# Layer 0's first four groups gathered during the node stage, a gather ring of eight, logit products in two halves

## The chip, the cores and the metric

The kernel runs on one core of one Trainium2 chip. The metric is the device time of one execution in microseconds; the time of a kernel is the median of several executions.

## The reference

Two graph layers over 12500 nodes (128 features, fp32) and 200000 edges that are sorted by destination:

```
xl, xr = x @ W_l, x @ W_r                       # by node; heads: 4 x 32
e      = sum_c leaky_relu(xl[src] + xr[dst]) * att
p      = exp(e - max over dst)                  # with a self loop for each node
out    = segment_sum(p / denom * xl[src], dst) + bias + x
x1     = layernorm(x + layernorm(out) * gamma + beta)
neigh  = segment_sum(x1[src] + edge_attr, dst)  # layer 1
out    = layernorm(x1 + leaky(( 2*x1 + neigh) @ W1 + b1) @ W2 + b2)
```

## The kernel before, in words

**Node stage.** 100 blocks of 128 nodes are handled in 50 pairs. SyncE loads x, TensorE turns it (`across`) and multiplies it with `w_lr` (`product`), ScalarE copies out, VectorE makes the self logits, SyncE stores `xl_table` (xl and four linear numbers for each node, DW = 132 wide) and `xr_table`. GpSimd prepares constants and then adds four numbers to `e_self` for each pair (`add_linear`).

**Sweep of layer 0.** The edges lie in 196 groups of 1024 (8 tiles of 128; the last group has 3 tiles), 1563 tiles in all. For each tile GpSimd issues one indirect DMA that gathers 128 rows of `xl_table` into `rows[s]`, a ring of U = 4 groups; it waits for the group's source numbers (`src_in0`) and for the slot (`rows_free0`, which VectorE gives in `weigh`). For each group TensorE turns the gathered rows (`sources`), adds the target rows by a one-hot product (`targets`, L804), multiplies with the attention vectors (`attend`, L830), and sums the weighted rows of the group before (`sum_up`, L846), which needs VectorE's one-hot (`edge_one_hot`, L1247). VectorE does the running maxima (`maxima`, `across`, `shift`) and the weighting (`weigh`, L1214). In every fourth group a window of 256 nodes is merged and written to `x1_table` (`merge_*`). Each engine has its own program, written out for four groups in a hardware loop (`sweep`), and the engines meet in semaphores alone. The order of TensorE in one step is: `sources(g+1)`, the turns of the maxima, `targets(g+1)`, `sum_up(g-1)`, `attend(g+1)`.

**Layer 1.** The same walk over 196 groups, with gathers of `x1_table` (L1588), behind a barrier of all engines.

Of the kernel before, what the change touches and what calls it, by code (L numbers as in the profile page):

```python
# [50 lines left out]
AHEAD = 3  # L51
# [39 lines left out]
def sweep(eng, groups, step, ends=None, layer=0, back=1):  # L91

    def part(tag, j, first, steps, lo, n):
        regs = []
        if ends is not None:
            regs = [eng.alloc_register(f"ends{layer}_{tag}_{k}") for k in range(2 * n)]
            eng.load(regs, ends[0:1, bass.ds(2 * first if j is None else j * (2 * U), 2 * n)])
        for c in steps:  # L100
            step(Group(j, c), lambda g: (regs[2 * (g.c - lo)], regs[2 * (g.c - lo) + 1]))

    part("head", None, 0, range(back), 0, max(2, back))
    with eng.Fori(0, groups // U - 1) as j:
        part("body", j, 0, range(back, U + back), 0, U + max(2, back))
    base = groups - U
    part("tail", None, base, range(base + back, groups + back), base, U)
# [67 lines left out]
def build(nc, a, out, edges, groups, blocks):  # L175
    nodes, real = blocks * P, REAL
    pairs = blocks // 2
    assert groups % U == 0 and groups > U and pairs % UP == 0 and pairs > UP
# [10 lines left out]
    with ctx:  # L189
# [48 lines left out]
        src_idx = [sb(f"src_idx{s}", [P, T], I32) for s in range(U)]  # L238
# [42 lines left out]
        near_row = pT2[:, T * NA:T * NA + P]  # L281
# [36 lines left out]

        row_slots = slots(rows[0]) + slots(rows[1]) + slots(rows[2]) + slots(rows[3])
# [22 lines left out]
        with nc.Block() as block:  # L342
            @block.sync
            def _(sp):
                for t, n in ((w_lr[:, 0:D], "W_l"), (w_lr[:, DW:DW + D], "W_r")):
                    sp.dma_start(t, a[n]).then_inc(S("products_in"), 16)

                def load(q):
                    if q.at_least(2 * R):
                        sp.wait_ge(S("x_taken"), q.times(1, 1 - 2 * R))  # L350
                    s = q.c % (2 * R)
                    sp.dma_start(ring_x[s], x_pair[q.times(1)]).then_inc(S(f"x_in{s}"), 16)

                def store(q):
                    s = q.c % R
                    if q.j is None and q.c < AHEAD:
                        sp.dma_start(src_idx[q.c][:, :], bass.AP(a["src"].tensor, q.c * G, [[T, P], [1, T]]))\
                          .then_inc(S(f"src_in0{q.c}"), 16)
# [10 lines left out]
            def _(pool):  # L369
# [29 lines left out]
                def add_linear(q):  # L399
                    pool.wait_ge(S("self_summed"), q.times(1, 1))  # L400
                    e_of = e_self_pair[:, q.times(1)]
                    pool.tensor_tensor(e_of, e_of, ring_w[q.c % R][:, :, D:DW], ALU.add).then_inc(S("e_made"), 1)

                node_loop(pool, pairs, [(add_linear, 0)])
# [33 lines left out]
            def _(act):  # L438
# [22 lines left out]
                def copy_out(q):  # L461
                    s = q.c % R
                    act.wait_ge(S("lr_ready"), q.times(1, 1))
                    if q.at_least(R):
                        act.wait_ge(S(f"xl_out{s}"), q.use(16, 0, R))
                        act.wait_ge(S("e_made"), q.times(1, 1 - R))
# [9 lines left out]
            def _(v):  # L476
# [51 lines left out]
                v.wait_ge(S("e_made"), pairs)  # L528
# [46 lines left out]
        def merge_of(g):  # L575

            return Group(g.j, (g.c - 1) // U, 1)
# [46 lines left out]
        def weights_in(v, k0, k1, link):  # L624
# [4 lines left out]
            tmp, own, self_ = msets[:, k0:k1, at_tmp:at_tmp + 2 * H], pair[:, :, 0, :], pair[:, :, 1, :]  # L629
            link(v.tensor_scalar(by_node(tmp), den, 0.0, -BIG, ALU.is_le, ALU.mult))  # L630
            link(v.tensor_tensor(by_node(own), su[:, :, :, H * HC:WC], by_node(tmp), ALU.add))
# [60 lines left out]
        def load_sources(sp, g):  # L692

            s, n = g.c % U, tiles(g)
            sp.wait_ge(S("src_taken0"), g.times(1, 2))
# [3 lines left out]
        with nc.Block() as block:  # L699
            @block.sync  # L700
            def _(sp):
                base, n, n_more, home = (sp.alloc_register(r) for r in ("sp_base", "sp_n", "sp_n_more", "sp_home"))
                sp.reg_mov(n_more, 0)

# [4 lines left out]
                def step(g, near):  # L709
# [34 lines left out]
                    if g.at_least(1) and not (g.j is None and g.c + AHEAD - 1 >= groups):  # L744
                        load_sources(sp, g + (AHEAD - 1))

# [5 lines left out]
                for s in range(BACK):  # L752
                    sp.wait_ge(S(f"rows_free0{s}"), groups // U + 1)
                    sp.dma_start(src_idx[s][:, :], bass.AP(a["src"].tensor, s * G, [[T, P], [1, T]]))\
# [3 lines left out]
            def _(pool):  # L758
                tables_stored(pool, ("xl",))
                def gather(s, n):  # L760
                    for t in range(n):
                        pool.indirect_dma_start(rows[s][:, t, 0:DW], None, xl_table[:, :],  # L762
                                                bass.IndirectOffsetOnAxis(ap=src_idx[s][:, t:t + 1], axis=0))\
# [7 lines left out]
                for s in range(U):  # L771
                    wait_alone(pool, pool_waits, S(f"src_in0{s}"), 16 * (groups // U))
                    wait_alone(pool, pool_waits, S(f"rows_free0{s}"), groups // U)
                    gather(s, tiles(Group(None, groups - U + s)))

            @block.tensor
            def _(pe):
# [10 lines left out]
                def sources(g):  # L788

                    s, h = g.c % U, ph[0]  # L790
                    wait_alone(pe, pe_waits, S(f"gathered0{s}"), g.use(16 * T, 16 * tiles(g)))
                    if g.at_least(1):
                        pe.wait_ge(S("relu_ready"), g.times(2, 0))
                    for t in range(tiles(g)):
                        pe.matmul(h[:, t, :], rows[s][:, t, 0:D], ident[:, :], start=(t % 4 == 0), stop=False,  # L795
# [26 lines left out]
                def attend(g):  # L822

                    if g.at_least(1):
# [1118 lines left out]
```

## Time and profile before

| | |
|---|---|
| median of 3 runs | 4075.12 us (4073.79 to 4075.89) |
| profiled execution: time | 4078.24 us |
| profiled execution: span of the trace | 4076.4 us |
| node stage | until 77 us |
| gathers of layer 0 | 77.5 to 2044 us |
| gathers of layer 1 | 2098 to 4062 us |
| busy share PE / DVE / ACT / GpSimd | 75% / 52% / 39% / 73% |
| granted TensorE clock, mean | 0.892 |

The shares are averages over three stages with different limits, so they don't say what bounds any of them. What counts is the spacing of GpSimd's gathers, and who waits for whom in each stage.

### The profile page before, as it was taken

What the parts mean: (1) busy time and instruction counts of PE and PEld (TensorE: products, weight loads), DVE (VectorE), ACT (ScalarE), POOL (GpSimd) and SP (SyncE); (2) the same over time, 40 slices, a digit from 0 to 9 for tenths busy, and PEclk for the clock granted to TensorE, in tenths of its full rate; (3) what the DMA queues carried; (4) which work ended last, traced back from release to release, by engine and by line L of the source; (5) the groups of instructions that cost most, each with busy time, mean ns of one, the idle gap of its engine ahead of it and who ended that gap; (6) DMA issues with size and microseconds to landing.
All of it is one profiled execution on the core that took longest, in us unless ns stands there. A gap on an engine that the chain in (4) does not pass through costs nothing. (4 is left out here: it accounts for less than half of the span.)

```text
span 4076.4 us, 80602 instructions
## 1 busy us (share of the span) xinstructions
PE 3042.1 (75%) x19237; PEld 2546.8 (62%) x19238; DVE 2101.4 (52%) x8183; ACT 1598.5 (39%) x3438; POOL 2993.8 (73%) x3200
## 2 busy tenths in 40 slices
PE   7888888888888888888846666666666666666666
PEld 6666666666666666666636666565666665666665
DVE  6777777777777777777743222222222222322222
ACT  5555555555565655555612212112121212121111
POOL 3777777777777777777737777777777777777776
PEclk9999999999999999999978888888888888888888
DMA  7545455554555454545444444444444444444443
GB/s 232 141 130 137 133 136 133 135 133 133 135 134 137 132 135 130 135 130 136 131 89 124 117 118 117 117 117 122 118 117 117 117 118 119 121 117 118 117 117 92
DMA packets 446506, 518.24 MB, mean 127 GB/s; under 512 B 198373, under 2 KB 346536, under 8 KB 446472
## 3 DMA queue, kind: packets, MB, share of 16 engines
q1 hardware_dynamic: 266390, 268.21, 21.7%
q0 software_dynamic: 100032, 208.27, 21.5%
q10 hardware_dynamic: 80050, 41.37, 3.6%
q8 instruction: 14, 0.23, 0.0%
q14 instruction: 20, 0.16, 0.0%
HBM read 470.23 MB, written 47.29 MB: 127 GB/s over the span
## 5 line engine op out<-in xcount | busy, mean ns | idle before, releaser
L1588 POOL DMA_INDIRECT rows<-x_table,src_idx x1563 | 1487.3, 952 | 530.0 <-issue 530.0
L762 POOL DMA_INDIRECT rows<-xl_table,src_idx x1563 | 1489.6, 953 | 479.0 <-issue 456.7
L846 PE MATMUL pA<-wmsg,edge_of 128*128 128x136 f32 x3126 | 405.6, 283 | 123.7 <-DVE edge_of L1247 123.1
L989 ACT ACTIVATE relu_h<-ph 128x512 f32<-128x512 f32 x391 | 231.3, 597 | 616.0 <-PE ph L804 616.0
L1611 PE MATMUL pA<-edge_of,dst_row 128*128 128x128 f32 x1568 | 304.0, 373 | 226.1 <-DMA rows<-x_table,src_idx 215.9
L846 PEld LDWEIGHTS pA<-wmsg,edge_of 128*128 128x128 f32 x3126 | 379.1, 190 | 134.5 <-issue 131.6
L1718 ACT ACTIVATE relu_h<-ph,b 128x128 f32<-128x128 f32 x196 | 72.0, 367 | 976.3 <-PE ph L1668 864.0
L1611 PEld LDWEIGHTS pA<-edge_of,dst_row 128*128 128x128 f32 x1568 | 283.4, 279 | 241.6 <-issue 240.9
L1611 PE MATMUL pT<-node_of,dst_row 128*128 128x128 f32 x1558 | 294.4, 367 | 181.2 <-DMA rows<-x_table,src_idx 172.1
L804 PE MATMUL ph<-node_of,xr_win 128*128 128x512 f32 (+1 forms) x782 | 411.8, 652 | 7.0 <-issue 6.6
L1044 ACT ACTIVATE node_of<-dst_row,first_node 128x1024 f32<-128x1024 int32 x196 | 405.5, 2069 | 2.4 <-DVE first_node L1158 2.4
L1611 PEld LDWEIGHTS pT<-node_of,dst_row 128*128 128x128 f32 x1558 | 274.1, 273 | 196.1 <-issue 195.2
L830 PE MATMUL pT<-att_heads,relu_h 128*128 128x48 f32 x3126 | 368.2, 271 | 0.0
L830 PEld LDWEIGHTS pT<-att_heads,relu_h 128*128 128x128 f32 x3126 | 364.6, 192 | 5.4 <-ACT relu_h L989 0.6
L795 PE MATMUL ph<-ident,rows 128*128 128x128 f32 x1563 | 225.6, 291 | 132.2 <-DMA rows<-xl_table,src_idx 131.5
L1663 PE MATMUL ph<-ident,relu_h 128*128 128x128 f32 x196 | 66.0, 337 | 326.5 <-DVE relu_h L1833 274.9
L1828 DVE TENSOR_TENSOR xr<-xr,pA 128x128 f32 x98 | 28.3, 288 | 540.2 <-PE pA L1611 537.3
L795 PEld LDWEIGHTS ph<-ident,rows 128*128 128x128 f32 x1563 | 180.7, 148 | 182.9 <-issue 181.1
L1247 DVE TENSOR_TENSOR edge_of<-dst_rel,pT 128x1024 f32<-128x1024 f32 x196 | 238.7, 1218 | 96.6 <-DVE dst_rel L1244 85.3
L1798 DVE TENSOR_TENSOR node_of<-sums,ph 128x1024 f32<-128x1024 f32 x98 | 119.0, 1214 | 274.8 <-issue 205.8
L1663 PEld LDWEIGHTS ph<-ident,relu_h 128*128 128x128 f32 x196 | 27.7, 141 | 363.6 <-DVE relu_h L1833 303.9
L1051 ACT ACTIVATE node_of<-node_of,one 128x1024 f32<-128x1024 f32 x196 | 224.5, 1145 | 61.5 <-issue 61.4
(207 smaller groups left out, 5454.4 us busy)
## 6 DMA issues: line engine op xcount, KB each, us to landing
dst_row<-in_dst SPq DMA_DIRECT2D x195, 513.0 KB
dst_row<-in_edge_attr SPq DMA_DIRECT2D x195, 512.0 KB
rows<-xl_table,src_idx POOLq DMA_INDIRECT x1563
rows<-x_table,src_idx POOLq DMA_INDIRECT x1563
sums_table<-win ACTq DMA_DIRECT2D x196, 68.0 KB
xr_win<-xr_table SPq DMA_DIRECT2D x196, 64.0 KB
relu_h<-x_table SPq DMA_DIRECT2D x196, 64.0 KB
out_x<-relu_h ACTq DMA_DIRECT2D x193, 64.0 KB
```

The lines of the kernel that those rows point to most:

```text
L762: pool.indirect_dma_start(rows[s][:, t, 0:DW], None, xl_table[:, :], bass.IndirectOffsetOnAxis(ap=src_idx[s][:, t:t + 1], axis=0))\
L795: pe.matmul(h[:, t, :], rows[s][:, t, 0:D], ident[:, :], start=(t % 4 == 0), stop=False, is_transpose=True)
L804: return [pe.matmul(h[:, k:min(k + 4, tiles(g)), :], xr_of[:, :], by_tile[:, k:min(k + 4, tiles(g)), :], start=False, stop=stop) for k in ...
L830: ins = pe.matmul(out_t[:, t, :], relu_h[0][:, t, :], att_heads[:, :], start=(t == 0), stop=(t == tiles(g) - 1))
L846: ins = pe.matmul(pA[k][:, 0:WC], edge_of[k][:, t, :], w[:, t, :], start=(t == 0), stop=(t == tiles(g) - 1))
L989: act.activation(relu_h[0][:, k:to, :], ph[0][:, k:to, :], ACT.Relu, scale=1.0 - GAT_SLOPE)\
L1044: act.activation(in_tiles(node_of[g.c % 2], tiles(g)), ids, ACT.Abs, scale=-1.0, bias=first_node[:, s:s + 1])\
L1051: act.activation(of, of, ACT.Relu, scale=-1.0, bias=one[:, :]).then_inc(S("node_of_made"), 1)
L1247: one_hot = lambda k: v.tensor_tensor(edge_of[k][:, 0:n_of, :], dst_rel[:, 0:n_of].unsqueeze(2).to_broadcast([P, n_of, P]), near_row.unsqu ...
L1588: pool.indirect_dma_start(rows[s][:, t, 0:D], None, x1_table[:, :], bass.IndirectOffsetOnAxis(ap=src_idx[s][:, t:t + 1], axis=0))\
L1611: ins = pe.matmul(bank, m[:, t, :], one_hot[:, t, :], start=(k == 0 and t == 0), stop=(k == 1 and t == n - 1))
L1798: return v.tensor_tensor(of[:, 0:n, :], rel[:, 0:n].unsqueeze(2).to_broadcast([P, n, P]), row_bank.unsqueeze(1).to_broadcast([P, n, P]), A ...
```

## The change

The source numbers of groups 0 to 3 are loaded at the very start. In the node stage GpSimd no longer runs `add_linear`; behind its constants it gathers the rows of **x** (not of `xl_table`) for groups 0 to 3, 32 indirect DMAs into `pre_rows`, a part of the tile `sums`. At the head of layer 0, TensorE and VectorE turn these rows and multiply them with `w_lr[:, 0:132]` in 16 pairs of tiles, and VectorE writes the products back over the rows. GpSimd's gathers from `xl_table` begin with group 4. `pre_rows` then serves as four more slots: the ring is eight deep (RING = 8), and so is the ring of source numbers. The loops of the sweep are written out for eight groups, not four. `attend` is split: the first four tiles' products are issued ahead of `sum_up`, the last four behind it. The linear part of the self logit is added by VectorE in the merge (one instruction more in `weights_in`). `near_row` moves from PSUM tile `pT2` to `ph[1]`, with two waits of VectorE on the merge.

```diff
-                def add_linear(q):
-                    pool.wait_ge(S("self_summed"), q.times(1, 1))
-                    ...
+                for k in range(U):
+                    pool.wait_ge(S(f"src_in0{k}"), 16)
+                    for t in range(T):
+                        pool.indirect_dma_start(pre_rows[:, k, t, 0:D], None, a["x"][:, :],
+                                                bass.IndirectOffsetOnAxis(ap=src_idx[k][:, t:t + 1], axis=0))\
+                            .then_inc(S(f"gathered0{U + k}"), 16)
```

```diff
+                for k in range(U):
+                    load_numbers(k)
...
-                with pool.Fori(0, groups // U - 1) as j:
-                    for s in range(U):
-                        wait_alone(pool, pool_waits, S(f"src_in0{s}"), j * 16 + 16)
-                        wait_alone(pool, pool_waits, S(f"rows_free0{s}"), j + 1)
-                        gather(s, T)
+                with pool.Fori(0, (groups - U) // RING - 1) as j:
+                    for c in range(U, U + RING):
+                        gather(Group(j, c, RING))
```

```diff
-                for _ in range(24):
-                    pe.matmul(pA[0][:, 0:P], ident[:, :], ident[:, :], start=True, stop=True)
+                def turn_pre(k):
+                    ...
+                    for b in range(2):
+                        ins = pe.transpose((pT1, pT2)[k % 2][:, b * P:(b + 1) * P], pre_rows[:, g, t + b, 0:D], ident[:, :])
+                def multiply_pre(k):
+                    ...
+                    for b in range(2):
+                        ins = pe.matmul(lr_bank[k % 2][:, b, 0:DW], pre_x[k % len(pre_x)][:, b, :], w_lr[:, 0:DW],
+                                        start=True, stop=True)
+                for k in range(len(pre_pairs) + 1):
+                    if k < len(pre_pairs):
+                        turn_pre(k)
+                    if k >= 1:
+                        multiply_pre(k - 1)
...
+                    if beyond:
+                        attend(g + 1, 0)
                     if g.at_least(1):
                         sum_up(g + -1, near(g + -1))
                     if beyond:
-                        attend(g + 1)
+                        attend(g + 1, 1)
```

```diff
+                def convert(first, last):
+                    for k in range(first, last):
+                        if k < len(pre_pairs):
+                            v.wait_ge(S("x_taken"), pairs + k + 1)
+                            v.tensor_copy(pre_x[k % len(pre_x)], (pT1, pT2)[k % 2][:, 0:2 * P]...)
+                        if k >= 1:
+                            v.wait_ge(S("lr_ready"), pairs + k)
+                            v.tensor_copy(pre_rows[:, g, t:t + 2, 0:DW], lr_bank[(k - 1) % 2][:, :, 0:DW])
...
                     if not g.at_least(1):
+                        half = len(pre_pairs) // 2
+                        convert(0, half + 1)
                         prepare(g)
                         first_of(g)
+                        convert(half + 1, half + 5)
                         homes_of_merges()
                         first_of(g + 1)
+                        convert(half + 5, 2 * half + 1)
                         starts_of_steps()
...
+                    if merge_phase(g) == 1:
+                        v.wait_ge(S("m_b_normed"), merge_of(g).times(1, 1))
```

## Rows read from the trace of the kernel before

**Rows 1.** The page: costliest groups; busy, mean ns | idle before, releaser.

```profile
L762 POOL DMA_INDIRECT rows<-xl_table,src_idx x1563 | 1489.6, 953 | 479.0 <-issue 456.7
```

**Rows 2.** Instructions of L762, with first and last start, and what ended its idle time.

```profile
L762 POOL DMA_INDIRECT rows<-xl_table,src_idx x1563: 947/952/1257, 77.5 to 2043.2; - x196
...
  DVE wmsg L1214: 9.8, 32
```

**Rows 3.** Instructions on the tile rows: ns min/median/max, first and last start.

```profile
L795 PE MATMUL ph<-ident,rows x1563: 272/273/472, 92.0 to 2053.3; 128*128 128x128 f32 x196
...
L1588 POOL DMA_INDIRECT rows<-x_table,src_idx x1563: 947/952/1628, 2098.2 to 4060.6; - x196
```

**Rows 4.** Waits from 140 to 2040 us: who for whom, total us, times, longest.

```profile
PE pA L846 <- DVE edge_of L1247: 121.8, 123, 1.1
PE ph L795 <- DMA rows<-xl_table,src_idx: 117.5, 103, 1.9
```

**Rows 5.** Windows: length, busy PE PEld DVE ACT POOL, clock, DMA share, GB/s.

```profile
40.00:60.00 20.00, 18.80 (x94) 14.55 (x93) 17.59 (x47) 14.29 (x46) 3.00 (x15) 1.00 0.81 250
...
80.00:100.00 20.00, 12.44 (x68) 10.18 (x66) 5.11 (x29) 8.21 (x9) 15.16 (x16) 0.76 1.03 301
...
500.00:1000.00 500.00, 434.39 (x2751) 329.56 (x2751) 371.69 (x1558) 293.37 (x607) 378.71 (x399) 0.97 0.51 134
```

**Rows 6.** Timeline of GpSimd, node stage and start of layer 0: start, us.

```profile
13.65 0.90 POOL L396 COPY att_heads<-att_col 32x1 f32<-32x1 f32 x4
...
77.49 1.21 POOL L762 DMA_INDIRECT rows<-xl_table,src_idx  x1 [1.93 <-issue]
...
109.21 0.95 POOL L762 DMA_INDIRECT rows<-xl_table,src_idx  x1 [1.32 <-DMA src_idx<-in_src]
```

**Rows 7.** Timeline, first microseconds of the kernel.

```profile
1.64 3.75 SPq L352 DMA_DIRECT2D rows<-in_x  x8
...
5.43 0.44 SPq L357 DMA_DIRECT2D src_idx<-in_src  x1
...
5.54 1.10 PE L415 MATMUL pT<-ident,rows 128*128 128x128 f32 x4 [5.54 <-DMA rows<-in_x]
```

**Rows 8.** The page's DMA queues: packets, MB, share of 16 engines.

```profile
q0 software_dynamic: 100032, 208.27, 21.5%
...
q8 instruction: 14, 0.23, 0.0%
q14 instruction: 20, 0.16, 0.0%
```

**Rows 9.** Node stage, 0 to 78 us: a wait, and a store's time to landing.

```profile
ACT edge_of L467 <- DMA xl_table<-edge_of: 1.8, 3, 1.2
...
xl_table<-edge_of SPq DMA_DIRECT2D x50, 132.0 KB, 2.6
```

**Rows 10.** Timeline, end of the node stage and head of layer 0.

```profile
63.78 0.41 DVE L513 TENSOR_TENSOR dst_row<-edge_of,ph 128x256 f32<-128x256 f32 x1
...
64.18 0.38 PE L415 MATMUL pT<-ident,rows 128*128 128x128 f32 x2
...
64.39 1.06 PE L428 MATMUL ph<-w_lr,rows 128*128 128x260 f32 x4
...
76.95 8.25 PE L882 MATMUL pA<-ident 128*128 128x128 f32 x48 [4.03 <-PEq L342]
...
92.04 1.94 PE L795 MATMUL ph<-ident,rows 128*128 128x128 f32 x8 [6.19 <-DMA rows<-xl_table,src_idx]
...
108.16 0.16 DVE L1158 TENSOR_TENSOR first_node<-node_id,firsts 128x1 f32<-128x1 f32 x1 [2.43 <-DMA dst_row<-in_dst]
...
110.74 1.22 DVE L1214 TENSOR_TENSOR wmsg<-rows,pT 128x1024 f32<-128x1024 f32 x1 [0.89 <-ACT r_exp L1028]
```

**Rows 11.** Timeline, a merge's instruction and a slot's sources in mid sweep.

```profile
1042.61 0.17 DVE L631 TENSOR_TENSOR sums<-sums 128x8 f32<-128x8 f32 x1
...
1046.20 1.07 PE L795 MATMUL ph<-ident,rows 128*128 128x128 f32 x8 [1.17 <-DMA rows<-xl_table,src_idx]
```

More of the change, by code:

```diff
@@ L50 @@
 TAIL = 3
-AHEAD = 3
+RING = 2 * U
 class Group:
@@ L91, in sweep, with part @@
 def sweep(eng, groups, step, ends=None, layer=0, back=1):
-    def part(tag, j, first, steps, lo, n):
+    pool = []
+    def part(j, first, steps, lo, n):
         regs = []
         if ends is not None:
-            regs = [eng.alloc_register(f"ends{layer}_{tag}_{k}") for k in range(2 * n)]
-            eng.load(regs, ends[0:1, bass.ds(2 * first if j is None else j * (2 * U), 2 * n)])
+            while len(pool) < 2 * n:
+                pool.append(eng.alloc_register(f"ends{layer}_{len(pool)}"))
+            regs = pool[0:2 * n]
+            eng.load(regs, ends[0:1, bass.ds(2 * first if j is None else j * (2 * RING), 2 * n)])
         for c in steps:
[L101 to L107, printed above, removed]
+            step(Group(j, c, RING), lambda g: (regs[2 * (g.c - lo)], regs[2 * (g.c - lo) + 1]))
+    loops = (groups - back - (RING - 1)) // RING
+    done = RING * loops
+    part(None, 0, range(back), 0, max(2, back))
+    with eng.Fori(0, loops) as j:
+        part(j, 0, range(back, RING + back), 0, RING + max(2, back))
+    part(None, done, range(done + back, groups + back), done, groups - done)
 def walk(eng, tag, groups, step, back, extra=0, wants=(), unrolled=0):
@@ L177, in build @@
     pairs = blocks // 2
-    assert groups % U == 0 and groups > U and pairs % UP == 0 and pairs > UP
+    assert groups % U == 0 and groups > 2 * RING and (groups - U) % RING == 0 and pairs % UP == 0 and pairs > UP
     assert nodes - 2 * UP * P <= real <= nodes - SPAN
@@ L317, in slots, with row_slot @@
                     for k in range(0, G - 2 * width + 1, 2 * width)]
+        assert U * PITCH <= 3 * groups
+        pre_rows = sums[:, :, :].rearrange("p b k -> p (b k)")[:, 0:U * T * PITCH].rearrange("p (s t k) -> p s t k", s=U, t=T)
+        rows_of_slot = [t[:, :, :] for t in rows] + [pre_rows[:, s] for s in range(U)]
+        pre_pairs = [(g, t) for g in range(U) for t in range(0, T, 2)]
+        pre_x = [relu_h[1][:, t:t + 2, :] for t in range(0, T, 2)]
+        def row_slot(g):
+            return (g.c + U) % RING
         row_slots = slots(rows[0]) + slots(rows[1]) + slots(rows[2]) + slots(rows[3])
@@ L703, in _ @@
                 sp.reg_mov(n_more, 0)
+                for k in range(U):
+                    sp.wait_ge(S(f"gathered0{U + k}"), 16 * T)
                 def window(first):
@@ L794, in sources @@
                     for t in range(tiles(g)):
-                        pe.matmul(h[:, t, :], rows[s][:, t, 0:D], ident[:, :], start=(t % 4 == 0), stop=False,
+                        pe.matmul(h[:, t, :], rows_of_slot[s][:, t, 0:D], ident[:, :], start=(t % 4 == 0), stop=False,
                                   is_transpose=True)
```

116 lines of the change are left out of this document (68 added, 48 removed).

## Prediction

> **What bounds the kernel now.** I read the page's costliest groups first, then the two gather lines by themselves, then the waits of the layer 0 stretch, and last the timelines where the stages meet. The costliest line of layer 0 is GpSimd's gather [rows 1]: its 1563 instructions keep the engine busy for 953 ns each, and nearly all of the idle time between them is "issue", which means that GpSimd waited for nobody. The source view says the same with a first and a last start [rows 2]: 1562 steps in 2043.2 - 77.5 = 1965.7 us, or 1.258 us a tile and 10.07 us a group of eight. Only 32 of them followed a wait for VectorE's `weigh`, 0.3 us each, no longer than the usual pause. So from 77.5 us on the sweep is as long as GpSimd's list of gathers. Layer 1 has the same list once more [rows 3] and isn't touched.
>
> The other engines have a little room. From 140 to 2040 us, some 189 groups, TensorE waited 117.5 us for gathered rows, 0.62 us a group, and 121.8 us (0.64 us a group) for the one-hot ahead of `sum_up` [rows 4]. Without the first wait a group would take them about 9.45 us. TensorE is busy 434 of 500 us there and VectorE 372 [rows 5], so the room isn't large.
>
> **The change part by part.**
>
> *32 gathers leave the list.* Groups 0 to 3 are 32 tiles, 32 x 1.258 = 40.3 us. If the first `xl_table` gather still starts at 77.5 us and GpSimd never waits, the last one starts 40.3 us earlier. What follows the last gather (layer 1's first gather starts 55 us behind it [rows 2, 3]) hangs on the last groups and merges, and moves along if the other engines have caught up by then. They have: at 9.45 us a group, 196 groups from about 105 us end near 1960 us, ahead of GpSimd's new end near 2005 (2043.2 less this term, and the others below). Term: -40.3.
>
> *The numbers of group 4.* GpSimd waited 1.32 us for them once [rows 6], against the usual 0.3. With eight slots they are loaded long before. Term: -1.0.
>
> *Source numbers at the start.* Four loads now stand in SyncE's queue ahead of the first load of x. One takes 0.44 us to issue [rows 7], so the first x starts 1.76 us later, and TensorE's first turn waited for exactly that load until 5.54 us [rows 7]. Nothing hides it; the node stage then runs at VectorE's pace and doesn't make it good. Term: +1.7 (0 if the ramp absorbs it, 2.0 at most). Four more loads stand ahead of the first stores; the stores' ring of five pairs covers them.
>
> *32 gathers in the node stage.* GpSimd is through its constants at 14.5 us [rows 6] and then has nothing but `add_linear`, 3.0 of 20 us [rows 5], which goes. 32 x 1.258 = 40.3 us, so it is done near 55 us, 22 us ahead of need. The cost is DMA traffic. The gathers' queue took 21.5% of 16 engines' span for 3126 gathers [rows 8], or 0.28 us of all engines for each. Spread at 1.258 us that adds 0.22 to a share of 0.81 [rows 5], which makes 1.03. The head of layer 0 shows just that share, at 301 GB/s against 250 here [rows 5], so it can be carried, but landings get longer. A store lands after 2.6 us, the ring gives it five pairs (about 6 us), and so far ScalarE waited 1.8 us in all for one [rows 9]. Bounds: 0, and 32 x 0.28 = 9.0 us if the engines were full and every gather pushed the stage back. I take +1.5, near the lower end, since the observed wait is small.
>
> *The product at layer 0's head.* A pair of tiles takes TensorE two turns (0.38 us) and two products of 132 columns, half of the 260-column pair's 1.06 us [rows 10], so 0.9 us; at the low clock of this stretch (mean 0.76 [rows 5]) up to twice that: the turns of eight tiles at 92 us took 1.94 us, in mid sweep 1.07 [rows 10, 11]. VectorE has two copies of about 0.42 us each (as L513 for 256 columns [rows 10]). With hand-overs I take 1.1 us a pair, 1.4 over the first four, and 3 us for VectorE's own head work in between: 77 + 16 x 1.2 + 3 = 99 us. TensorE's cover goes: the 24 warming products (8.25 us [rows 10]) and the wait for the first gather until 92.0 us were idle time that this fills. From there `sources(0)`, `targets(0)`, `attend(0)`, the maxima and `shift` take about 13 us, so `weigh(0)` ends near 112 us. The step before also ended there for another reason: VectorE waited for `dst_row` until 108.16 us and `weigh(0)` ran from 110.74 to 111.96 [rows 10]; that load stands behind the stores of `xr_table` in SyncE's program, as it will after the change. GpSimd needs slot 4 free only for its 33rd gather, at 77.5 + 40.3 = 117.8 us. So 6 us are spare. Term: 0, with bounds 0 and +8 (at 2 us a pair `weigh(0)` ends at 125 us).
>
> *Half the products ahead of `sum_up`.* Four tiles' products now run in the 0.64 us a group in which TensorE waits for the one-hot [rows 4]. That shortens TensorE's step by up to as much, but GpSimd sets the pace. Term: 0 in the sweep.
>
> *One more instruction in the merge* (0.17 us and its wait [rows 11], about 0.2) lies in one step of four, within the room; once it is behind the last group: +0.2. VectorE's new wait for `m_b_normed` is for work that ScalarE does at the end of its step before, and VectorE gets to the place only behind TensorE's turns of the next step: 0; what is queued behind it is the one-hot, for which TensorE's `sum_up` waits. If room were gone, 49 x 0.2 = 10 us would be the bound.
>
> *Loops of eight groups.* The profile counts 1558 VectorE instructions in 500 us [rows 5], 31 a group; a pass of eight has 250, and semaphore, register and branch instructions on top. The code that a loop needs is fetched once today: 34 packets of instructions in the whole span [rows 8], against 48 passes of each loop. What a jump costs when code isn't there is bounded by TensorE's 4.03 us at the entry into layer 0 [rows 10]. In 23 passes, one of 80.5 us each, a stall of 4.03 us meets room of 8 x 0.62 = 5.0 us. Term: 0.
> The Trainium skill (Runtime: NRT & Kernel Launch, section Instruction fetch mechanics) says that an engine other than TensorE holds 512 instructions, and that a taken branch out of that window stalls for a fetch. By it VectorE's pass of eight, if it holds over 512, would stall at each back edge where the pass of four shows no fetch; the trace of before has no loop that long and can't decide it. The sum would be the same as long as the room covers the stall.
>
> **Sum.** -40.3 - 1.0 + 1.7 + 1.5 + 0.2 = -37.9 us. The profiled execution took 4078.2 us (span 4076.4 and 1.8 around it), which gives 4040.3. The median of the runs shown is 3.1 us below that execution, so I forecast 4075.1 - 37.9 = 4037.2, say 4037 us.
>
> **Rivals.**
> - *Late handover.* VectorE and TensorE need 1.7 to 2.2 us a pair, `weigh(0)` ends after 118 us and GpSimd waits up to 8 us at its 33rd gather: 4038 to 4045. For it: the low clock at the head, and a chain of four hand-overs a pair. Against: 6 us of spare time.
> - *The node stage is pushed back* by the added traffic, 3 to 9 us in place of 1.5: 4039 to 4045. For it: share 0.81 before. Against: 1.03 was carried elsewhere.
> - *The list of gathers isn't what matters*: the other engines can't go faster than 10.07 us a group, and the head start is lost, since their last step comes when it came. 4075, no change. The 117.5 us of TensorE's waits for gathers speak against it.
> - *A stall in each pass of the longer loops* (slower). VectorE or TensorE fetches code at each back edge. It costs nothing up to 5 us a pass, and 23 us for each further microsecond; 37.9 / 23 = 1.65, so from 6.7 us a pass on the kernel is slower than before. At 8 us, two stalls as at the entry: 4037 + 69 = 4106. Against it: one such stall is 4 us, and the halved products leave TensorE another 0.6 us a group.
>
> **How the numbers follow.** Forecast as summed (4030 to 4043): 0.61. Late handover 0.13. Node stage pushed back 0.13. A stall that eats part of the gain (4045 to 4067) 0.04. No change 0.04, slower by the stall 0.05. What a measurement of this kernel can tell from no change is about 0.2%, 8 us. Faster takes the first three and most of the fourth, 0.90; within 0.2% 0.05; slower 0.05. The first rivals together reach 4053; below 4030 nothing in the sum leads (no start-up loss and no traffic cost give 4034). Range 4030 to 4054.
>
> **What the profile will show.** 1531 gathers from `xl_table`, first near 79 to 81 us (the node stage is 1.7 + 1.5 us longer), 1.258 us apart, last start near 2005 us. Layer 1's first gather 55 us behind it. 32 gathers of x between 15 and 56 us. TensorE's waits for gathered rows in the sweep no smaller than before, and its wait for the one-hot nearly gone. GpSimd waits for `weigh` at most once. Wrong if: GpSimd shows waits for `weigh` in each pass; a gap in VectorE's or TensorE's list every 80 us with instruction packets beside it; or the first `xl_table` gather starts past 85 us.

## The result, and the profile after

The changed kernel takes 4108.87 us (median; 4108.34 to 4116.3), the kernel before took 4074.45 us beside it: ratio 1.0088, 95% interval 1.0071 to 1.0106. It is 34 us slower. 4037 had been forecast, so 72 us are to be explained. The profiled execution is the slowest of the four (4116.3 us, span 4114.7), 7 us above the median, so differences of spans and starts between the two profiles come out some us larger than the 34.

First GpSimd's gathers, with first and last start, and what ended GpSimd's idle time (the name is that of the tile that holds the slot):

```profile
L789 POOL DMA_INDIRECT rows<-xl_table,src_idx x768: 947/952/1121, 81.5 to 2008.2; - x192
L789 POOL DMA_INDIRECT sums<-xl_table,src_idx x763: 946/952/1206, 121.9 to 2042.2; - x191
...
  issue: 484.9, 1445
  DVE wmsg L1274: 39.7, 86
```

There are 1531 gathers from `xl_table` in place of 1563, and the first starts at 81.5 us, near the 81 forecast. But the last starts at 2042.2 us, where it was before [rows 2], not near 2005. The list is 32 gathers shorter and as long in time. GpSimd now waits for VectorE's `weigh` 86 times. The logits, and layer 1's first gather (2098.2 us before [rows 3]), show that the layer as a whole ends later still:

```profile
L1262 DVE TENSOR_TENSOR logits<-pT,sums x100: 164/202/205, 105.0 to 2099.6; 128x32 f32<-128x32 f32 x99, 128x12 f32<-128x12 f32 x1
```

```profile
L1658 POOL DMA_INDIRECT rows<-x_table,src_idx x1563: 947/952/2234, 2137.4 to 4100.8; - x196
```

195 steps in 1994.6 us are 10.23 us a group. Before, the same line ran from 98.7 to 2062.3 us, 10.07 a group. Layer 1 is 39 us later at its start and 1 us longer in itself. So nearly all of the loss in these two profiles lies in layer 0's sweep (31 us) and ahead of it (6 us).

Who waits for whom there, 140 to 2040 us (total us, times, longest), against [rows 4]:

```profile
PEld pT L951 <- DVE run L1266: 130.6, 82, 4.1
DVE logits L1262 <- issue: 126.3, 23, 5.8
PE pT L951 <- DVE run L1266: 107.3, 78, 3.9
```

TensorE's waits for gathered rows and for the one-hot have gone from the head of the list. In their place it waits for `run`, the softmax scan of VectorE, and VectorE stands 23 times, 5.5 us each, ahead of the logits with nothing in the profile that it waits for. There are 23 passes of the longer loop. In the kernel before this row read 63.0 us in 47 times, 1.3 us each (reading a pass's registers and branching). The timelines of VectorE, ScalarE and TensorE around one of the 23:

```profile
1020.82 0.17 DVE L702 SCALAR_TENSOR_TENSOR sums<-sums 128x2 f32<-128x2 f32 x1
1026.59 0.20 DVE L1262 TENSOR_TENSOR logits<-pT,sums 128x32 f32<-128x32 f32 x1 [5.60 <-issue]
```

```profile
1022.71 0.34 ACTq L1017 DMA_DIRECT2D x_table<-sums  x1
1028.14 0.37 ACTq L629 DMA_DIRECT2D sums<-sums_table  x1
```

```profile
1022.47 1.97 PE L818 MATMUL ph<-ident,sums 128*128 128x128 f32 x8 [1.96 <-issue]
1027.36 0.37 PE L951 MATMUL pT<-ident,run 128*4 128x128 f32 x1 [2.93 <-DVE run L1266]
...
1028.01 3.78 PE L827 MATMUL ph<-node_of,xr_win 128*128 128x512 f32 x4
...
1038.65 1.55 PE L827 MATMUL ph<-node_of,xr_win 128*128 128x512 f32 x3 [0.19 <-issue]
```

VectorE's last instruction of the pass starts at 1020.82 us and the first of the next at 1026.59. The views leave out branches and register loads, but the trace has their records: VectorE's branch back ends at 1021.35 us, its next record of any kind starts at 1024.97, and the load of the pass's registers takes another 1.35 us. This gap behind the branch, 3.6 us in the median of 23 passes (2.7 us on ScalarE, 0.1 on TensorE), is what "gap" means below; before the change it is 0.3 us on VectorE and 0.2 on ScalarE. ScalarE issues nothing between 1023.1 and 1028.1 us. TensorE runs out of work and waits for `run`; after that the four matmuls of `targets` take 3.78 us; three of them take 1.55 us at the full clock (last line), so four need about 2. Windows around this stall (length, busy PE, granted clock, DMA share, GB/s) show why: in the second the clock is at the lower of its two levels (1.2 GHz in place of 2.4), behind TensorE's two waits, and in the third at the upper one again.

```profile
1012.00:1020.00 8.00, 7.53 (x52) 1.00 0.52 152
1025.00:1032.00 7.00, 4.58 (x8) 0.50 0.44 110
1036.00:1044.00 8.00, 7.44 (x43) 1.00 0.46 123
```

What came in the meantime is in the DMA queues, packets and MB, of the whole page and of the window 300 to 1000 us:

```profile
q14 instruction: 296, 2.42, 0.2%
q8 instruction: 23, 0.38, 0.0%
```

```profile
q14 instruction: 99, 0.81, 0.4%
```

99 packets of instructions in mid sweep, 8.2 KB each, about 12 for each pass of 82 us. Before, the same window had none, and the whole span 34 [rows 8]. This is the rival "A stall in each pass of the longer loops", and two of the prediction's three signs of being wrong are there: waits for `weigh` in each of five passes looked at, and VectorE's gap every 80 us with instruction packets beside it. The third isn't, since the first gather starts before 85 us.

What a pass pays shows in the steps from the start of one group's logits to the next, by their place in the pass (means of 21 passes). Before, the step that holds VectorE's branch took 11.8 us. Now it takes 15.8, 4 us more, and the step in the middle of the pass, which no longer has a branch and a load of registers, takes 10.1, 1.6 us less. So the stall arrives in full, and the longer loop gives back a good third of it.

### The profile page after: what moved, and what is told of

It reads as the page before. It is cut to its first block and busy times, and to the rows that moved or that the text cites. A ratio compares the mean times of both kernels' runs of the same rounds, so it can differ in the third digit from the quotient of the medians.

```text
span 4114.7 us, 79626 instructions
## 1 busy us (share of the span) xinstructions
PE 3116.4 (76%) x19285; PEld 2585.2 (63%) x19286; DVE 2115.6 (51%) x8265; ACT 1601.8 (39%) x3438; POOL 2990.2 (73%) x3150
## 5 line engine op out<-in xcount | busy, mean ns | idle before, releaser
L789 POOL DMA_INDIRECT sums<-xl_table,src_idx x763 | 732.1, 960 | 263.6 <-issue 234.6
L789 POOL DMA_INDIRECT rows<-xl_table,src_idx x768 | 732.2, 953 | 261.0 <-issue 250.3
L827 PE MATMUL ph<-node_of,xr_win 128*128 128x512 f32 (+1 forms) x782 | 429.2, 676 | 17.0 <-issue 11.0
L870 PE MATMUL pA<-wmsg,edge_of 128*128 128x136 f32 x3126 | 419.7, 289 | 6.6 <-DVE edge_of L1307 5.6
L853 PE MATMUL pT<-att_heads,relu_h 128*128 128x48 f32 x3126 | 411.5, 276 | 12.9 <-ACT relu_h L1041 12.9
L853 PEld LDWEIGHTS pT<-att_heads,relu_h 128*128 128x128 f32 x3126 | 392.9, 196 | 25.3 <-ACT relu_h L1041 13.8
L870 PEld LDWEIGHTS pA<-wmsg,edge_of 128*128 128x128 f32 x3126 | 387.5, 195 | 13.8 <-issue 8.3
L1307 DVE TENSOR_TENSOR edge_of<-dst_rel,ph 128x1024 f32<-128x1024 f32 x196 | 238.7, 1218 | 104.6 <-DVE dst_rel L1304 104.6
L827 PEld LDWEIGHTS ph<-node_of,xr_win 128*128 128x128 f32 x782 | 146.1, 208 | 165.6 <-issue 149.8
```

The lines of the kernel that those rows point to most:

```text
L789: pool.indirect_dma_start(rows_of_slot[s][:, t, 0:DW], None, xl_table[:, :], bass.IndirectOffsetOnAxis(ap=src_idx[k][:, t:t + 1], axis=0))\
L827: return [pe.matmul(h[:, k:min(k + 4, tiles(g)), :], xr_of[:, :], by_tile[:, k:min(k + 4, tiles(g)), :], start=False, stop=stop) for k in ...
L853: ins = pe.matmul(out_t[:, t, :], relu_h[0][:, t, :], att_heads[:, :], start=(t == 0), stop=(t == tiles(g) - 1))
L870: ins = pe.matmul(pA[k][:, 0:WC], edge_of[k][:, t, :], w[:, t, :], start=(t == 0), stop=(t == tiles(g) - 1))
L1307: one_hot = lambda k: v.tensor_tensor(edge_of[k][:, 0:n_of, :], dst_rel[:, 0:n_of].unsqueeze(2).to_broadcast([P, n_of, P]), near_row.unsqu ...
```

## The experiments

The instructions of a pass, counted in the programs: VectorE 314 before and 619 after, ScalarE 158 and 310, TensorE 327 and 644 (752 and 1494 with a matmul in fp32 counted as several). A pass holds more than it executes: `further_windows` is a loop for groups that span several windows, and its body, never entered with these inputs, stands in the code as often as the group does.

**Shorter loops, one engine and then all.** Edit: the `further_windows` loops of layer 0 are left out, so that groups that span several windows would not be computed; in the first run VectorE's two alone, in the second also ScalarE's, TensorE's and SyncE's.

```diff
                     wait_alone(v, v_waits, S("first_made"), g.times(1, 1))
-                    further_windows(v, n, span, further)
...
-                    further_windows(v, n, span, further)
                     one_hot(0).then_inc(S("edge_of_made"), 1)
```

> The changed kernel with the never-entered inner loops for groups wider than 128 nodes taken out of VectorE's layer 0 program alone (leaves out the handling of such groups; these inputs have none). VectorE's pass of eight groups shrinks from 619 to 386 instructions in the program; what it executes is nearly the same. Theory A (the pass of eight is too long for what VectorE holds, so it fetches code and stalls at each back edge, about 5 to 6 us in every 82 us pass): VectorE's gap at the back edge goes, GpSimd sets the pace again, 4030 to 4050 us. Theory B (other engines' step got longer through the split products, the moved near_row and the merge's extra instruction): 4100 to 4110, as the changed kernel. Theory C (it is ScalarE's or TensorE's longer pass that stalls): 4090 to 4110.

> The same inner loops taken out of all engines' layer 0 programs (VectorE 386, TensorE 965 in place of 1494, ScalarE 210 in place of 310, SyncE 88 in place of 176 instructions a pass; leaves out the handling of groups wider than 128 nodes, of which these inputs have none). Theory A: the same as with VectorE's alone, 4030 to 4050 us, unless 386 instructions still don't fit for VectorE. Theory C: this one is fast, 4030 to 4050, and the one with VectorE's alone is not. Theory B: 4095 to 4110.

Measured: VectorE alone (386 instructions a pass) 4090.4 us, ratio 1.0036 (1.0022 to 1.005); all engines (VectorE 386, ScalarE 210, TensorE 965, again with matmuls counted as several) 4056.43 us, 0.9939 (0.9918 to 0.996). In 300 to 1000 us the packets fall from 99 to 83 and 44:

```profile
q14 instruction: 83, 0.68, 0.3%
```

```profile
q14 instruction: 44, 0.36, 0.2%
```

Leaving these loops out of all engines moves the time by 52 us, and the second kernel is faster than the one before. Not all of it is shorter code. The register and branch instructions around the loops go too: their busy time falls from 1.12 to 0.39 us a group on TensorE and from 1.04 to 0.59 on VectorE. And 386 instructions aren't short enough for VectorE: behind its branch back there is still a gap of 2.95 us (3.6 in the changed kernel), and yet this kernel is as fast as the one below in which no engine stalls. How the 52 us divide between stall and register work isn't shown by these two runs. ScalarE's gap of 2.8 us is there with 310 instructions and gone with 210. The Trainium skill (Runtime: NRT & Kernel Launch, section Instruction fetch mechanics) gives these engines 512 instructions, refilled in blocks of 256, and a stall for a taken branch out of that window. The stall is as the page has it. As a limit on the length of a loop the 512 don't hold here, since loops of 386 and 310 are stalled; the packets are of 8.2 KB, half of the page's 16 KiB blocks. Where in a block each loop begins was neither recorded nor varied, so what the limit depends on isn't shown.

**The long loop without the change.** Edit: the kernel before, with 38 (then 16) memsets in each of VectorE's eight never entered bodies. No instruction more is executed.

```diff
                         v.reg_add(n_hide, n_hide, 1)
+                        for _ in range(38):
+                            v.memset(warm[:, :], 0.0)
...
                         v.reg_add(n_sum, n_sum, 1)
+                        for _ in range(38):
+                            v.memset(warm[:, :], 0.0)
```

> The kernel before, with 38 memsets put into each of VectorE's eight never-entered inner loops of layer 0: nothing more is executed, only the code of a pass of four groups grows from 314 to 622 instructions. Theory A: instruction packets appear in every pass of 40 us, VectorE stalls 5 to 6 us at each back edge, room is 2.5 us, so a pass becomes 43 to 44 us and the kernel takes 4074 + 48 x 3 to 4, 4200 to 4270 us. Theory B: 4074, no change.

> The same with 16 memsets in each: 446 instructions a pass. Theory A with a limit of 512 instructions: no instruction packets in the loop and 4074 us, no change; if the code is held in blocks and the pass now touches one block too many, as slow as the longer one (4200 to 4270). Theory B: 4074.

Measured: 622 instructions a pass, 4231.39 us, 1.0379 (1.0362 to 1.0397); 446 a pass, 4201.78 us, 1.0309 (1.0292 to 1.0326). Their loops have 48 passes, so the price is (4231.4 - 4076.5) / 48 = 3.2 us and 2.6 us a pass. In 300 to 1000 us there are 113 and 82 instruction packets where the kernel before has none, and the gap behind VectorE's branch is 2.9 and 3.0 us in place of 0.3. The wait of the long one, and its gathers:

```profile
DVE logits L1204 <- issue: 177.0, 44, 4.4
```

```profile
L762 POOL DMA_INDIRECT rows<-xl_table,src_idx x1563: 946/952/1214, 77.4 to 2194.1; - x196
```

4.0 us each in place of 1.3, so the stall itself is 2.7 us, and all or nearly all of it arrives in the time of both (the step with the branch takes 14.7 and 14.5 us in place of 11.8). That the two prices differ by 0.6 us at the same gap isn't explained. The kernel before had no room for a stall either. The gathers that were to set the pace were themselves held back, from 2043 to 2194 us.

**A hint for the branch.** Edit: in the changed kernel the branches back of VectorE's and ScalarE's loops of eight groups are announced by a prefetch hint. In the trace it is the first instruction of each pass, so it stands some 80 us ahead of the branch that it announces.

```diff
-    with eng.Fori(0, loops) as j:
+    hinted, slotted = ('DVE', 'Activation'), {}
+    e = eng.engine
+    with eng.bass.Fori(0, loops, engines=OrderedEngineSet([e]), hint_back_edge=str(e).split('.')[-1] in hinted,
+                       ...
```

> The changed kernel, with a hint ahead of the branch back in VectorE's and ScalarE's loops of eight groups, so that the code at the loop's head is asked for before the branch is taken; one more instruction in each pass, nothing else differs. Theory A (the branch back stalls for code: 3.6 us of VectorE and 2.8 us of ScalarE in each of 23 passes, and what follows from it): if the hint hides it all, the gaps at the branch fall below 1 us and the time is 4035 to 4055; if the hint only starts the fetch a few instructions early, the gap shrinks by less than 1 us and the time stays at 4090 to 4108. As many instruction packets as before in either case, or more. Theory B (the sweep is slower because the other engines' steps are, with no part for code): no change, 4105 to 4112.

Measured: 4098.65 us, 1.006 (1.0043 to 1.0077): 10 us better than the changed kernel and still slower than before, so neither of the two outcomes written down. The gap behind VectorE's branch falls to 1.15 us, ScalarE's below 0.6, and the packets of 300 to 1000 us from 99 to 51. But the row of VectorE's idle time has only halved:

```profile
DVE logits L1266 <- issue: 67.1, 23, 3.9
```

It is 2.9 us each, with 1.3 to 1.5 where no stall is. The step with the branch is 2.4 us shorter than in the changed kernel (13.4 against 15.8), as much as the gap. But the other seven steps of a pass are 1.4 us longer together. The branches that skip the never entered loops, 16 in a pass of VectorE, show a gap of 0.27 us behind them in place of 0.15, here and in the next run with a hint, which is 1.9 us a pass. So with the hint VectorE's other branches took longer, and that most likely eats what the shorter stall won; why they do, and why 1.15 us of stall remain, isn't settled.

**ScalarE's loop short, VectorE's long.** Edit: `sweep` gets a length, and ScalarE's is four groups; then the same with the hint on VectorE.

```diff
-def sweep(eng, groups, step, ends=None, layer=0, back=1):
+def sweep(eng, groups, step, ends=None, layer=0, back=1, ring=None):
...
-                sweep(act, groups, step, spans)
+                sweep(act, groups, step, spans, ring=U)
```

> The changed kernel, with ScalarE's loop alone written out for four groups again (159 instructions a pass in place of 310); VectorE's and TensorE's stay at eight. Theory A: ScalarE's 2.8 us gap goes, instruction packets fall from about 12 to about 7 for each pass of eight groups, VectorE's gap of 3.6 us stays. If ScalarE's stall adds to VectorE's, 4085 to 4100; if it lies beside it (both branch at about the same time), 4103 to 4110. Theory B: no change and no fewer packets.

> The kernel with ScalarE's loop of four groups, and the hint on VectorE's loop of eight. Theory A with a hint that works: 4035 to 4055, as the run with both hints; if the hint does nothing, as the run with ScalarE's loop of four alone. Theory B: 4105 to 4112.

Measured: 4145.03 us, 1.0169 (1.0152 to 1.0186), and 4134.57 us, 1.0147 (1.013 to 1.0164). A miss: a stall was taken away and the kernel got 36 us slower. ScalarE's gap and its packets are gone as expected (57 packets in 300 to 1000 us), and the step with VectorE's branch is as long as before it (15.9 against 15.8 us): beside VectorE's stall, ScalarE's cost nothing. What came is this, in the waits and in both timelines:

```profile
DVE sums L653 <- DMA sums<-sums_table: 45.1, 23, 2.8
```

```profile
1001.50 0.37 ACTq L630 DMA_DIRECT2D sums<-sums_table  x1
...
1005.61 0.17 DVE L653 TENSOR_SCALAR sums<-sums 128x8 f32<-128x8 f32 x1 [1.96 <-DMA sums<-sums_table]
```

A merge begins every four groups. In its step ScalarE issues the load of the sums, which VectorE waits for before its `weigh`. With ScalarE's branch back now ahead of every such step, the load is issued about 1.2 us later (4.9 us behind the store ahead of it, against 3.6 in the middle of a pass of eight). VectorE has no branch there that holds it back as well, so 23 times it waits 2 us for the landing. 45 us of wait stand against 36 us of time. The first two experiments had this wait too (94.2 and 66.1 us), which is part of why they gained no more.

**Both loops short.** Edit: VectorE's loop is four groups as well. It needs the slot of eight from a register that is swapped each pass, the rows and sums in one tile, and one counting semaphore for free slots. All that the change does is kept: ring of eight, gathers ahead, products in halves.

```diff
-        rows = [sb(f"rows{s}", [P, T, PITCH]) for s in range(U)]
+        store = sb("rows_and_sums", [P, U * T * PITCH + blocks * WC])
+        all_rows = store[:, 0:RING * T * PITCH].rearrange("p (s t k) -> p s t k", s=RING, t=T)
...
+                def rows_of(g):
+                    if g.j is None:
+                        return rows_of_slot[row_slot(g)]
+                    half = v.snap(far_half, ...) if g.c == U else v.snap(near_half, ...) + g.c
+                    return all_rows[:, bass.ds(half, 1)].rearrange("p s t k -> p (s t) k")
...
-                sweep(v, groups, step, spans)
+                sweep(v, groups, step, spans, ring=U)
```

> The changed kernel with all that it does (ring of eight, 32 gathers ahead, product at layer 0's head, logit products in two halves), but VectorE's and ScalarE's loops written out for four groups (324 and 159 instructions a pass): the slot of the rows comes from a register that is swapped each pass. TensorE, SyncE and GpSimd keep loops of eight. Theory A: no instruction packet in mid sweep, no gap at the branch, gathers 1.258 us apart as in the kernel before, and 4033 to 4045, which is what the prediction gave for the change without a stall. Theory B (the two halves of the products, or the ring, slow the steps): 4075 or more, with TensorE's and VectorE's steps at 10 us or more a group and no packets.

> The kernel with short loops once more, in more rounds, as the best version so far: 4050 to 4063 us beside 4076 of the kernel before, ratio 0.994 to 0.997.

Measured: 4058.82 us (4045.21 to 4065.3), ratio 0.9948 (0.9929 to 0.9968); again, on another chip, 4063.46 us, 0.9966 (0.9954 to 0.9978). VectorE's pass has 324 instructions, ScalarE's 159, and the page has 23 packets in all on the queue that had 296, none of them in mid sweep. So the short loops win 4108.9 - 4058.8 = 50 us (45 by the other run), 2.2 us for each of 23 passes. This is a net price: the stalls go, while VectorE loads its registers twice as often and has the work of the swapped slots on top (the register and branch instructions take 1.38 us a group in place of 1.04). Both steps of eight that hold VectorE's branch take 11.9 us, as before the change. This version beats both kernels. Its gathers, and its logits:

```profile
L792 POOL DMA_INDIRECT rows_and_sums<-xl_table,src_idx x1531: 947/952/1208, 79.2 to 2004.5; - x192
```

```profile
L1274 DVE TENSOR_TENSOR logits<-pT,rows_and_sums x196: 164/202/206, 102.2 to 2048.2; 128x32 f32<-128x32 f32 x195, 128x12 f32<-128x12 f32 x1
```

The last gather starts at 2004.5 us, and 2005 was the forecast. But the logits end at 2048.2 us, 44 us behind it; before the change it was 19 us (2062.3 - 2043.2). They take 9.98 us a group (9.96 in mid sweep) with the rows long there, where the prediction had 9.45. TensorE's waits, which the prediction had counted as free time, are others now:

```profile
PE pT L954 <- DVE run L1278: 90.3, 65, 2.0
...
PE ph L821 <- issue: 45.4, 23, 2.0
```

So 22 us were still open: the price of the halves, or the other engines' own pace.

**The halves undone, the halves alone, GpSimd delayed.** Edits: the kernel with short loops, with both halves behind `sum_up`; the kernel before, with the halves and the two waits and the place of `near_row` that they need; the kernel with short loops, with 20 memsets ahead of GpSimd's first gather from `xl_table`.

```diff
-                    if beyond:
-                        attend(g + 1, 0)
                     if g.at_least(1):
                         sum_up(g + -1, near(g + -1))
                     if beyond:
+                        attend(g + 1, 0)
                         attend(g + 1, 1)
```

```diff
+                idling = Chain(pool, S("idle_chain"))
+                for _ in range(20):
+                    idling.link(pool.memset(idle[:, :], 0.0))
```

> The kernel with short loops (VectorE's and ScalarE's written out for four groups), with the logit products whole again and behind the sums, as before the change. In the run with short loops GpSimd's last gather of layer 0 started at 2004.5 us, as forecast, but the logits took 9.98 us a group against 9.45 in the prediction's room, and the layer ended 19 us later than forecast. Theory H (the halves cost TensorE or VectorE time once gathers are no longer what they wait for): undoing them gives 9.6 us a group or less, and 4035 to 4045. Theory R (the halves are neutral, and 9.98 us is what the chain between VectorE, ScalarE and TensorE needs, with or without them): 9.9 to 10.1 us a group and 4052 to 4066. If the halves helped: over 10.1 us a group and over 4070.

> The kernel before, with the logit products in two halves around the sums, and what comes with them (the row of near numbers in another PSUM bank, VectorE's wait for the merge's last scaling); ring of four, loops of four, no gathers ahead. The prediction's term was 0, since GpSimd sets the pace: 4072 to 4080, TensorE's wait for the one-hot falls from 0.64 us a group to under 0.2, its wait for gathered rows grows by as much. If the halves slow VectorE's chain by more than the room: over 4084.

> The kernel with short loops, with 20 memsets of 128x1024 on GpSimd, some 20 us, ahead of its first gather from xl_table; nothing else differs. Theory R (from the second dozen groups on the other engines set the pace, at 9.98 us a group, and GpSimd runs up to 44 us ahead of them at the end): the last gather starts 15 to 20 us later, but the time grows by at most 8 us, 4052 to 4067. Theory P (GpSimd still sets the pace): all of the delay shows, 4075 to 4085.

These three, and a repeat of each, ran on a chip on which the kernel before itself took 5898 and 5952 us, so they price nothing (first time 5973.24, 6074.65 and 6143.98 us, second 6049.99, 5984.06 and 6088.42). On sound chips:

> The kernel with short loops, logit products whole again and behind the sums; third time, the two calls before ran on a disturbed chip. Theory H (the halves cost time once gathers aren't waited for): 9.6 us a group or less and 4035 to 4045. Theory R (9.98 us a group is what the chain between VectorE, ScalarE and TensorE needs, with or without halves): 9.9 to 10.1 us a group and 4052 to 4066. If the halves helped: over 4070.

> The kernel with short loops, with 20 memsets of 128x1024 on GpSimd, some 20 us, ahead of its first gather from xl_table; third time, for the same reason. Theory R (the other engines set the pace): last gather 15 to 20 us later, time 4052 to 4067. Theory P (GpSimd still sets the pace): all of the delay shows, 4075 to 4085.

> The kernel before, with the logit products in two halves around the sums and what comes with them; ring of four, loops of four, no gathers ahead. With the halves undone, the kernel with short loops went from 4058.8 to 4078.1 us, so there they are worth 19 us. Here GpSimd's list of gathers (77.5 to 2043 us) is what the layer waits for, by the prediction, and the term was 0: 4072 to 4080, with the last gather where it was and TensorE's wait for the one-hot under 0.2 us a group. If the own pace of the other engines set the time in the kernel before as well: 4055 to 4065.

Measured, halves undone: 4078.05 us, 1.0006 (0.9996 to 1.0015), which is the time of the kernel before. The halves are worth 4078.1 - 4058.8 = 19 us here (15 by the other run), so the theory that they cost something falls, and so does the one that they are neutral. The logits, and TensorE's wait for the one-hot, which is back:

```profile
L1273 DVE TENSOR_TENSOR logits<-pT,rows_and_sums x196: 165/203/208, 101.5 to 2070.7; 128x32 f32<-128x32 f32 x195, 128x12 f32<-128x12 f32 x1
```

```profile
PE pA L873 <- DVE edge_of L1318: 110.5, 112, 1.2
```

1969.2 / 195 = 10.10 us a group, with no wait for gathers. The execution with this trace is the slowest of ten, 4093.2 us, 15 above their median. If all of that lay in this sweep, the median would have 1954.1 / 195 = 10.02 us a group, so the pace without the halves is between 10.02 and 10.10 (an estimate). GpSimd delayed: 4060.81 us, 0.9962 (0.9948 to 0.9976).

```profile
L793 POOL DMA_INDIRECT rows_and_sums<-xl_table,src_idx x1531: 947/952/1192, 99.4 to 2025.2; - x192
```

The gathers start 20 us later, and the time is 2 us above one run of the undelayed kernel and 3 below the other: behind the change GpSimd isn't what the sweep waits for. The halves alone on the kernel before: 4078.35 us, 1.0003 (0.9994 to 1.0012), first and last gather at 77.2 and 2043.5 us. There TensorE's wait for the one-hot is gone from the list and its wait for rows has grown from 117.5 to

```profile
PE ph L795 <- DMA rows<-xl_table,src_idx: 158.9, 137, 2.1
```

as the step "Half the products" had it.

## Why the prediction was wrong

The head of the layer, step by step, was right. The profile after, in order of time:

```profile
98.79 0.43 DVE L1181 COPY sums<-ph 128x264 f32<-128x264 f32 x1 [0.47 <-PE ph L920]
...
114.16 0.16 DVE L1219 TENSOR_TENSOR first_node<-node_id,firsts 128x1 f32<-128x1 f32 x1 [6.95 <-DMA dst_row<-in_dst]
117.60 1.22 DVE L1274 TENSOR_TENSOR wmsg<-sums,pT 128x1024 f32<-128x1024 f32 x1 [1.39 <-ACT r_exp L1080]
```

```profile
121.85 0.95 POOL L789 DMA_INDIRECT sums<-xl_table,src_idx  x1 [0.30 <-issue]
```

- *Source numbers and traffic in the node stage*, +1.7 and +1.5. Right as a sum: the first `xl_table` gather starts 4.0 us later (81.5 against 77.5), 3.2 were forecast; in the three kernels with short loops, which begin alike, it starts at 78.1 to 79.8. The split was off: TensorE's first turn starts 0.8 us later, not 1.7 (6.37 us against 5.54 [rows 7]), and the stage lost ground while the gathers ran (84 matmuls in 20 to 40 us where there were 99). The DMA share of 40 to 60 us rose from 0.81 [rows 5] to 0.92, and to 0.95 in the part of it in which gathers still ran (until 53.3 us), not to 1.03.
- *The product at the head*, 0. Right: the last conversion ends at 99.2 us (forecast 99). `weigh(0)` ends at 118.8, not 112, since `dst_row` landed 6 us later than before; GpSimd's 33rd gather at 121.85 us waited for nothing. The margin was 3 us, not 6.
- *32 gathers leave the list*, -40.3. The list behaves as forecast once nothing stalls (last gather 2004.5 us in the kernel with short loops). But the step went on: "They have: at 9.45 us a group, 196 groups from about 105 us end near 1960 us". That failed. 9.45 was got by taking TensorE's wait for rows off the 10.07, as if nothing else filled it. Measured with the rows there: 10.02 to 10.10 us without the halves, 9.98 with them. In the kernel before, GpSimd's list (10.07 a group) and the chain through VectorE, ScalarE and TensorE were about equally long: each of the two edits that shortens one of them wins nothing alone. That TensorE's two waits lay within that chain is argued from the rates, not shown by itself. So the term, with all loops short, was worth -17 us together with the halves (-13 by the other run), and nothing without them.
- *Half the products*, 0. Right by itself (ratio 1.0003), wrong beside the shorter list: there the halves carry all of the gain, 15 to 19 us. The two edits are worth nothing singly and 13 to 17 us together.
- *Loops of eight groups*, 0. This is the step that made the sign wrong: "a stall of 4.03 us meets room of 8 x 0.62 = 5.0 us". The stall came in each pass, within the size allowed for (3.6 us on VectorE, 2.7 on ScalarE), and the room wasn't there, for the reason above: the step with VectorE's branch grew by 4 us, the whole stall and a little more. The net price is 50 us (45 by the other run), 2.2 us a pass, since the longer loop also saves a branch and a load of registers in its middle step; in the kernel before, 2.6 to 3.2 us a pass. TensorE's clock is at half behind the stall shown, and its mean over 140 to 2040 us falls from 0.97 to 0.93. Part of that comes without any stall (0.95 with short loops, 0.96 with the halves alone), and what the rest costs wasn't measured.
- *One more instruction in the merge*, +0.2: not separated from the rest.

The two measured terms, -17 and +50, add up to the measured change by construction, since both are read against the kernel with short loops; what supports them is that the stall added alone to the kernel before costs as much and more a pass. The rival had the right mechanism and the threshold wrong: it was held to be free up to 5 us a pass. With room 0 its own formula gives about 23 us for each microsecond of stall, 83 us for 3.6; the 50 are less mainly because the middle step saves nearly 2 us a pass.

What stays open: why the hint leaves 1.15 us of the stall and lengthens other branches, what sets the pace of 9.96 us a group once neither gathers nor stalls do, and how far between 324 and 386 instructions VectorE's limit lies (or whether it depends on where the loop begins).

## What to carry to other kernels

When a loop that runs often is written out further, count the instructions of one pass on each engine, bodies that are never entered too, and compare with loops that show no instruction packets; in the profile after, look first at the instruction queue in a mid-loop window. A wait in the profile of a balanced kernel isn't spare time: what an engine could do without the wait is bounded by the longest chain through all engines, and delaying the supposed bottleneck (20 us of idle work on it) tests at small cost whether it is one. And in such a kernel two edits may be worth nothing each and something together, or a stall removed on one engine may cost time on another (36 us here), so judge them together.

## What the runs showed of the hardware

- Loops of 386, 446, 619 and 622 instructions a pass on VectorE and of 310 on ScalarE fetched code in every pass; loops of 314 and 324 on VectorE, 210 and 159 on ScalarE, fetched none. TensorE's with 1494 had no gap behind its branch (0.1 us).
- The fetch shows as instruction packets of 8.2 KB and a gap of 2.7 to 3.7 us behind the branch, larger than the packets' share of DMA time (0.4% in mid sweep) suggests.
- A prefetch hint for the branch back, issued at the head of each pass, shortened VectorE's gap from 3.6 to 1.15 us and ScalarE's from 2.7 to 0.2, and halved the packets (99 to 51 in 700 us); the gap behind VectorE's other branches grew from 0.15 to 0.27 us.
- One chip ran the same kernel in 5900 us in place of 4076. In the variants profiled there, VectorE and ScalarE waited some 70 times each, 10 to 14 us at a time, for things that the profile of this core doesn't show. Ratios between kernels weren't kept there: the kernel with the halves alone had 1.029 and 1.016 in place of 1.0003.
